# Last feed-forward part of a two-layer decoder: rows quantised by groups, rounding and conversion on ACT, tile stages spread over four steps

## The chip, the cores and the metric

The kernel runs on one core of a Trainium2 chip. The metric is the device time of one launch in microseconds (us), the median of several runs. One further execution was taken with the hardware profiler; all rows come from it.

## The reference

Two decoder layers work on x, 16 sequences of 64 rows of 256 columns in float32 (1024 rows). Layer 0 is a state-space block, a cross attention and a feed-forward part with two experts; layer 1 is an attention, a cross attention and the feed-forward part that the change touches. Each works on the layer norm of x and is added to x. The last one, with weights of 1024 x 256 (gate, up) and 256 x 1024 (down):

```
def _quant_weight(w):
    scale = mean(abs(w)) + EPS
    return clip(round(w / scale), -1, 1), scale
def _quant_act(x):
    s = max(abs(x), axis=-1) / 127 + EPS
    return clip(round(x / s), -128, 127), s
def _qlinear(x, w):
    wq, ws = _quant_weight(w);  xq, xs = _quant_act(x)
    return (xq @ wq.T) * xs * ws
h = silu(_qlinear(x, w_gate)) * _qlinear(x, w_up)
y = _qlinear(h, w_down)
```

## The kernel before, in words

Every engine has its own instruction list, written by hand; the engines meet only at semaphores. An instruction waits in its queue's order, and all that stands behind it on that engine waits too. `after(...)` on DVE and ACT makes the engine wait for its own instruction before the next. The 1024 rows lie in 8 tiles of 128 partitions (x[:, t, :]). PSUM has 8 banks of 2 KB a partition; `pair(a)` is banks a and a+1 as 1024 columns, `tiles2(a)` is bank a as two tiles of 256.

The last part begins where the second cross attention (`cross(1)`) ends. PE's project_out (L846) leaves two tiles each in banks 0 to 3 and signals x1_out once for each two.

Layer norm (`norm_rows(5, ...)`, DVE L1049 to L1063, ACT L380 and L381): for each group of two tiles DVE adds the bank to x, takes bn_stats and bn_aggr; ACT computes rstd with Ln and Exp; DVE scales group g-1 behind the statistics of group g.

Quantising the rows (DVE L1314 to L1323): once all 8 tiles are scaled, one maximum over all, two small instructions, a scale with minimum for each tile, one pass for maximum and adding MAGIC (1.5 x 2^23, which rounds), one pass for subtracting MAGIC and writing bf16, then the factors for gate and up (g_sc, u_sc). PE transposes (L1002) 8 tiles in two banks, ACT copies them out (L620) to t_xqT.

The tile loop runs over t from 0 to 8. In step t:
- PE (L1015): gate into pair(0), up into pair(2), 8 matmuls of 512 columns, once t_gate and t_prod say that tile t-1 has left these banks. Then for tile t-1: 8 transposes (L1022) of t_hq into bank 4, and after ACT's copy (t_hT) 8 down matmuls (L1029) into bank 5 or 6.
- ACT: Silu of the gate (L629), then the copy of bank 4 of tile t-1 to t_hqT (L633).
- DVE: product (L1330), maximum (L1334), its scale and reciprocal (L1335, L1336), scale with minimum (L1337), maximum and add MAGIC (L1338), subtract MAGIC to bf16 (L1341), down factor (L1342), and for tile t-1 the update of x from the down bank (L1345), which signals y_done.
- SP (L315) stores tile t of x on y_done.

In front of all this, weights t_gate, t_up and t_down have been loaded (DVE's 3 sums L1294) and quantised on POOL, long before. The kernel opens with four memsets on DVE. L426, L385 and L591 are ACT instructions of earlier parts.

## Time and profile before

| | us |
|---|---|
| median of 3 runs (lowest, highest) | 1158.2 (1157.13, 1160.88) |
| profiled execution, its own time | 1162.1 |
| its span | 1160.2 |
| PE, matmuls busy | 957.1 (82%) |
| DVE busy | 647.7 (56%) |
| ACT busy | 422.1 (36%) |
| POOL busy | 248.7 (21%) |

The span is what the trace shows from its first to its last event. Busy shares are averages over stages with different limits. In the rows, PE is the matmuls, PEld the weight loads, and the granted clock is a share of TensorE's full 2.4 GHz (0.50 is 1.2 GHz). `[2.69 <-DVE region_c L1330]` means that the engine had stood idle for 2.69 us and that this line's result ended it.

### The profile page before, as it was taken

What the parts mean: (1) busy time and instruction counts of PE and PEld (TensorE: products, weight loads), DVE (VectorE), ACT (ScalarE), POOL (GpSimd) and SP (SyncE); (2) the same over time, 40 slices, a digit from 0 to 9 for tenths busy, and PEclk for the clock granted to TensorE, in tenths of its full rate; (3) what the DMA queues carried; (4) which work ended last, traced back from release to release, by engine and by line L of the source; (5) the groups of instructions that cost most, each with busy time, mean ns of one, the idle gap of its engine ahead of it and who ended that gap; (6) DMA issues with size and microseconds to landing.
All of it is one profiled execution on the core that took longest, in us unless ns stands there. A gap on an engine that the chain in (4) does not pass through costs nothing.

```text
span 1160.2 us, 13033 instructions
## 1 busy us (share of the span) xinstructions
PE 957.1 (82%) x5454; PEld 597.4 (51%) x5458; DVE 647.7 (56%) x744; ACT 422.1 (36%) x632; POOL 248.7 (21%) x90
## 2 busy tenths in 40 slices
PE   4587787877879999999998999978863789999565
PEld 2133232322255566676666666647752467777332
DVE  2588789889942422333234344427768444444586
ACT  2653544542324655555452111142320313222232
POOL 0057586686600000000000000010009900000000
PEclk9788899988999999999998899987565989999777
DMA  8345454454614000000000500020000000000000
GB/s 304 86 128 141 108 146 130 109 145 125 183 62 174 1 1 1 1 1 1 1 1 1 208 0 1 1 108 3 3 5 0 1 1 1 1 1 2 0 14 23
DMA packets 17018, 64.43 MB, mean 56 GB/s; under 512 B 2848, under 2 KB 4512, under 8 KB 15456
## 3 DMA queue, kind: packets, MB, share of 16 engines
q1 hardware_dynamic: 16960, 63.60, 18.0%
q8 instruction: 43, 0.70, 0.3%
q14 instruction: 15, 0.12, 0.0%
HBM read 60.05 MB, written 3.15 MB: 54 GB/s over the span
## 4 chain that ended last, share of the span: by engine, by line
PE 63%; DVE 20%; ACT 7%; POOL 4%; issue 4%; DMA 1%; SPq 1%; DVEq 0%; POOLq 0%; ACTq 0%
PE ps L782 9%; PE ps L846 9%; DVE region_c L1138 6%; PE ps L888 5%; PE ps L702 5%; PE ps L898 5%; PE ps L657 4%; PE ps L814 3%; PE ps L836 3%; POOL region_c L347 3%; PE ps L800 3%; DVE ps L1133 2%; PE ps L796 2%; ACT region_c L565 2%; PE ps L789 1%
## 5 line engine op out<-in xcount | busy, mean ns | idle before, releaser
L702 PE MATMUL ps<-region_c,ident 128*128 128x512 f32 x256 | 141.4, 679 | 34.1 <-POOL region_c L347 25.0
L1138 DVE TENSOR_TENSOR_SCAN region_c<-region_c,ps 128x1024 f32<-128x1024 f32 x64 | 146.3, 2286 | 10.5 <-ACT region_c L470 8.5
L347 POOL TENSOR_TENSOR region_c<-region_c,region_b 128x1024 f32<-128x1024 f32 x43 | 105.0, 2442 | 110.4 <-DVE region_c L1138 103.2
L846 PE MATMUL ps<-region_c 128*128 128x256 f32 x512 | 117.5, 384 | 2.7 <-ACT region_c L565 2.7
L846 PEld LDWEIGHTS ps<-region_c 128*128 128x128 f32 x512 | 98.4, 193 | 27.4 <-issue 11.5
L470 ACT ACTIVATE region_c<-region_c,a_log 128x1008 f32<-128x1008 f32 x64 | 71.6, 1131 | 86.1 <-DVE region_c L1138 84.1
L356 POOL TENSOR_TENSOR x<-x,region_a 128x2048 f32<-128x2048 f32 x1 | 4.5, 4507 | 443.4 <-DVE xn L1049 443.4
L702 PEld LDWEIGHTS ps<-region_c,ident 128*128 128x128 f32 x256 | 50.4, 210 | 94.6 <-issue 47.3
L1133 DVE TENSOR_TENSOR ps<-ps,region_c 128x1024 f32<-128x1024 f32 x64 | 78.9, 1233 | 23.4 <-PE ps L690 18.4
L1200 DVE TENSOR_TENSOR region_c<-region_c 128x512 f32<-128x512 f32 x32 | 22.2, 692 | 119.8 <-ACT region_c L540 119.8
L565 ACT ACTIVATE region_c<-ps 128x512 f32<-128x512 f32 x64 | 36.9, 597 | 117.6 <-PE ps L836 117.6
L690 PE MATMUL ps<-region_b,sel_b 96*128 96x512 bf16 x128 | 41.1, 404 | 38.3 <-DVE ps L1133 32.5
L782 PE MATMUL ps<-xnT,region_a 128*128 128x512 f32 x128 | 60.7, 618 | 0.8
L888 PE MATMUL ps<-xnT,region_b 128*128 128x512 f32 x128 | 61.3, 605 | 0.0
L898 PE MATMUL ps<-region_b,region_c 128*128 128x256 f32 x256 | 60.1, 379 | 0.0
L836 PE MATMUL ps<-region_b,ctxn 64*128 64x128 f32 x512 | 56.7, 291 | 4.0 <-DVE region_b L1204 1.9
L782 PE MATMUL ps<-xnT,region_c 128*128 128x512 f32 x128 | 58.0, 598 | 0.8
L898 PEld LDWEIGHTS ps<-region_b,region_c 128*128 128x128 f32 x256 | 48.6, 190 | 19.4 <-issue 14.4
L523 ACT ACTIVATE region_c<-ps 128x512 f32<-128x512 f32 x64 | 37.9, 594 | 54.1 <-PE ps L782 54.1
L347 POOL TENSOR_TENSOR region_c<-region_c 128x1024 f32<-128x1024 f32 x21 | 51.4, 2446 | 27.9 <-DVE region_c L1138 23.3
L836 PEld LDWEIGHTS ps<-region_b,ctxn 64*128 64x128 f32 x512 | 50.5, 193 | 8.7 <-ACT region_c L565 5.2
L690 PEld LDWEIGHTS ps<-region_b,sel_b 96*128 96x128 bf16 x128 | 10.6, 102 | 85.7 <-DVE ps L1133 59.8
(188 smaller groups left out, 1535.7 us busy)
## 6 DMA issues: line engine op xcount, KB each, us to landing
region_b<-m_rows SPq DMA_DIRECT2D x43, 512.0 KB, 4.5
region_c<-m_rows SPq DMA_DIRECT2D x21, 512.0 KB, 4.6
region_a<-in_x_wo SPq DMA_DIRECT2D x2, 2048.0 KB, 12.0
m_rows<-region_b SPq DMA_DIRECT2D x4, 512.0 KB, 5.4
region_a<-in_x_wq SPq DMA_DIRECT2D x1, 2048.0 KB, 9.5
region_b<-in_f_fc SPq DMA_DIRECT2D x1, 2048.0 KB, 8.2
region_b<-in_f_proj SPq DMA_DIRECT2D x1, 2048.0 KB, 12.6
region_a<-in_x_wqT SPq DMA_DIRECT2D x1, 2048.0 KB, 14.6
```

The costliest lines, as they stand in the source:

```text
L347: pool.tensor_tensor(m_hc[u % 2], m_h[u % 3], m_cb[u % 3], ALU.mult).then_inc(sem("m_hc"), 1)
L470: act.activation(m_da[n % 2][:, :, 1:S], m_delta[k % 2][:, :, 1:S], ACT.Exp, scale=a_log[:, k, n:n + 1]).then_inc(sem("m_da"), 1)
L565: act.activation(dst, b.rearrange("p (a j n) -> p a j n", a=2, j=2), ACT.Copy)\
L690: last = pe.matmul(ps[:, c, :], sel_b[:, u % 32, :], m_sb[:, u // 32, c * HALF:c * HALF + HALF], start=True, stop=True)
L702: last = pe.matmul(ps[:, 4 + c, :], ident[:, :], m_hc[n % 2][:, c * HALF:c * HALF + HALF], start=(n == 0), stop=(n == DST - 1))
L782: last = pe.matmul(b, w, xnT[:, k, c * HALF:c * HALF + HALF], start=(k == 0), stop=(k == KH - 1))
L836: last = pe.matmul(b[:, :, m, :], ctxn[64 * r:64 * r + 64, js, :], mov, start=True, stop=True)
L846: last = pe.matmul(tiles2(t // 2)[:, t % 2, :], o_T[:, a, 128 * t:128 * t + 128], wvo[:, 2 * i + a, :], start=(i == 0 and a == 0 and t % 2 ...
L888: last = pe.matmul(ps[:, 4 + n % 4, :], f_fc[:, k, HID * e + 128 * hb:HID * e + 128 * hb + 128], xnT[:, k, c * HALF:c * HALF + HALF], star ...
L898: last = pe.matmul(tiles2(2 * e + t // 2)[:, t % 2, :], f_act[n % 4][:, 128 * t:128 * t + 128], f_proj[:, HB * e + hb, :], start=(hb == 0 ...
L1133: dve.tensor_tensor(pair(2), pair(0), m_du, ALU.mult).then_inc(sem("m_dbu"), 1)
L1138: dve.tensor_tensor_scan(m_h[u % 3], m_da[n % 2].rearrange("p b t -> p (b t)"), pair(2), 0.0, ALU.mult, ALU.add).then_inc(sem("m_scan"), 1)
```

## The change

Front: the last layer norm is written out. Behind the statistics of group g DVE runs scaled_rows(g-1) (scale, maximum, scales, factors, for these two tiles) and, later, clipped_rows. Rounding is now an ACT activation: Identity with the row's reciprocal scale as multiplier and MAGIC as addend, both read from `small`. DVE clips between MAGIC - 128 and MAGIC + 127 in one instruction, and a second ACT activation subtracts MAGIC and writes bf16. PE transposes by groups of two tiles, into banks 4 to 7, ACT copies by groups.

Loop: it runs over s from 0 to 11. In step s, gate and up, Silu, product and maximum are of tile s, rounding and clip of tile s-1, conversion to bf16 of tile s-2, transposes of tile s-3, copy, down matmuls and update of tile s-4. t_hqT and t_r have two buffers each; bank 4 stays the only one for transposes, and PE waits for the copy of the tile before (t_hT) ahead of them. The diff, in which longer runs of removed lines (they stand in the kernel above) are cut:

```diff
--- before.py
+++ after.py
@@ -200,8 +200,9 @@
         t_gate = [view("C", 16 + 4 * i, [HID]) for i in range(2)]
         t_h = [view("C", 24 + 4 * i, [HID]) for i in range(2)]
         t_hq = [view("C", 32 + 2 * i, [HID], BF16) for i in range(2)]
-        t_hqT = view("C", 36, [HB, 128], BF16)
-        t_r = view("C", 40, [HID])
+        t_hqT = [view("C", 36 + 2 * i, [HB, 128], BF16) for i in range(2)]
+        t_r = [view("C", 40 + 4 * i, [HID]) for i in range(2)]
+        magic_col, unmagic_col = small[:, 40:41], small[:, 41:42]
 
         def tiles2(a):
 
@@ -614,23 +615,66 @@
             norm_rows(4)
             cross(1)
 
-            norm_rows(5, transposed=False)
-            for g in range(2):
+            def rounded_rows(g):
+                act.wait_ge(sem("t_xs"), g + 1)
+                for t in (2 * g, 2 * g + 1):
+                    last = act.activation(t_xr[:, t, :], xn[:, t, :], ACT.Identity, scale=small[:, 32 + t:33 + t],
+                                          bias=magic_col)
+                last.then_inc(sem("t_xr"), 1)
+
+            def small_rows(g):
+                act.wait_ge(sem("t_xc"), g + 1)
+                act.activation(t_xq[:, 2 * g:2 * g + 2, :], t_xr[:, 2 * g:2 * g + 2, :], ACT.Identity,
+                               bias=unmagic_col).then_inc(sem("t_xq"), 1)
+
+            def turned_rows(g):
                 act.wait_ge(sem("t_xtr"), g + 1)
-                act.activation(t_xqT[:, :, HALF * g:HALF * g + HALF],
-                               ps[:, 2 * g, :].bitcast(BF16).rearrange("p (k n) -> p k n", k=KH), ACT.Copy)\
+                act.activation(t_xqT[:, :, 256 * g:256 * g + 256],
+                               ps[:, 4 + g, 0:256].bitcast(BF16).rearrange("p (k n) -> p k n", k=KH), ACT.Copy)\
                     .then_inc(sem("t_xT"), 1)
-            for t in range(NT + 1):
-                if t < NT:
-                    act.wait_ge(sem("t_gu"), t + 1)
-                    act.wait_ge(sem("t_sc"), 1)
+
+            for g in range(4):
+                act.wait_ge(sem("ln_var"), 4 * 5 + g + 1)
+                r = rstd[:, 2 * g:2 * g + 2]
+                after(act.activation(r, mv[:, 2 * g:2 * g + 2, 1], ACT.Ln, bias=eps_col))
+                act.activation(r, r, ACT.Exp, scale=-0.5).then_inc(sem("ln_rstd"), 1)
+                if g >= 2:
+                    rounded_rows(g - 2)
+            for g in range(4 + 1):
+                if g < 4:
+                    small_rows(g)
+                if g < 2:
+                    rounded_rows(g + 2)
+                if g >= 1:
+                    turned_rows(g - 1)
+
+            for s in range(NT + 4):
+                if s < NT:
+                    act.wait_ge(sem("t_gu"), s + 1)
+                    act.wait_ge(sem("t_sc"), s // 2 + 1)
+                    if s >= 2:
+                        act.wait_ge(sem("t_prod"), s - 1)
+                    act.activation(t_gate[s % 2], pair(0), ACT.Silu, scale=small[:, 56 + s:57 + s])\
+                        .then_inc(sem("t_gate"), 1)
+                if 1 <= s <= NT:
+                    t = s - 1
+                    act.wait_ge(sem("t_hr"), t + 1)
                     if t >= 2:
-                        act.wait_ge(sem("t_prod"), t - 1)
...
+                        act.wait_ge(sem("t_hq"), t - 1)
+                    act.activation(t_r[t % 2], t_h[t % 2], ACT.Identity, scale=small[:, 80 + t:81 + t],
+                                   bias=magic_col).then_inc(sem("t_round"), 1)
+                if 2 <= s <= NT + 1:
+                    t = s - 2
+                    act.wait_ge(sem("t_clip"), t + 1)
+                    if t >= 2:
+                        act.wait_ge(sem("t_htr"), t - 1)
+                    act.activation(t_hq[t % 2], t_r[t % 2], ACT.Identity, bias=unmagic_col).then_inc(sem("t_hq"), 1)
+                if s >= 4:
+                    t = s - 4
+                    act.wait_ge(sem("t_htr"), t + 1)
+                    if t >= 2:
+                        act.wait_ge(sem("t_dn"), t - 1)
+                    act.activation(t_hqT[t % 2], ps[:, 4, :].bitcast(BF16).rearrange("p (k n) -> p k n", k=HB),
                                    ACT.Copy).then_inc(sem("t_hT"), 1)
 
 
@@ -994,39 +1038,44 @@
             pe.wait_ge(sem("t_ws"), 1)
             cross(1)
 
-            for g in range(2):
-                pe.wait_ge(sem("t_xq"), 1)
-                xt = ps[:, 2 * g, :].bitcast(BF16).rearrange("p (k n) -> p k n", k=KH)
+            for g in range(4):
+                pe.wait_ge(sem("t_xq"), g + 1)
+                xt = ps[:, 4 + g, 0:256].bitcast(BF16).rearrange("p (k n) -> p k n", k=KH)
                 for k in range(KH):
-                    for t in range(4):
-                        last = pe.transpose(xt[:, k, 128 * t:128 * t + 128],
-                                            t_xq[:, 4 * g + t, 128 * k:128 * k + 128], identb[:, :])
+                    for a in range(2):
+                        last = pe.transpose(xt[:, k, 128 * a:128 * a + 128],
+                                            t_xq[:, 2 * g + a, 128 * k:128 * k + 128], identb[:, :])
                 last.then_inc(sem("t_xtr"), 1)
-            pe.wait_ge(sem("t_xT"), 2)
             pe.wait_ge(sem("t_wq"), 3)
-            for t in range(NT + 1):
...
+            pe.wait_ge(sem("t_xT"), 4)
+            for s in range(NT + 4):
+                if s < NT:
+                    if s >= 1:
+                        pe.wait_ge(sem("t_gate"), s)
+                        pe.wait_ge(sem("t_prod"), s)
                     for o, w in ((0, t_gate_q), (2, t_up_q)):
                         for c in range(2):
                             for k in range(KH):
-                                last = pe.matmul(ps[:, o + c, :], t_xqT[:, k, 128 * t:128 * t + 128],
+                                last = pe.matmul(ps[:, o + c, :], t_xqT[:, k, 128 * s:128 * s + 128],
                                                  w[:, k, 512 * c:512 * c + 512], start=(k == 0), stop=(k == KH - 1))
                     last.then_inc(sem("t_gu"), 1)
-                if t >= 1:
-                    pe.wait_ge(sem("t_hq"), t)
+                if 3 <= s <= NT + 2:
+                    t = s - 3
+                    pe.wait_ge(sem("t_hq"), t + 1)
+                    if t >= 1:
+                        pe.wait_ge(sem("t_hT"), t)
                     ht = ps[:, 4, :].bitcast(BF16)
                     for k in range(HB):
-                        last = pe.transpose(ht[:, 128 * k:128 * k + 128], t_hq[(t - 1) % 2][:, 128 * k:128 * k + 128],
+                        last = pe.transpose(ht[:, 128 * k:128 * k + 128], t_hq[t % 2][:, 128 * k:128 * k + 128],
                                             identb[:, :])
                     last.then_inc(sem("t_htr"), 1)
-                    pe.wait_ge(sem("t_hT"), t)
-                    if t >= 3:
-                        pe.wait_ge(sem("y_done"), t - 2)
+                if s >= 4:
+                    t = s - 4
+                    pe.wait_ge(sem("t_hT"), t + 1)
+                    if t >= 2:
+                        pe.wait_ge(sem("y_done"), t - 1)
                     for k in range(HB):
-                        last = pe.matmul(ps[:, 5 + (t - 1) % 2, 0:D], t_hqT[:, k, :], t_down_q[:, k, :],
+                        last = pe.matmul(ps[:, 5 + t % 2, 0:D], t_hqT[t % 2][:, k, :], t_down_q[:, k, :],
                                          start=(k == 0), stop=(k == HB - 1))
                     last.then_inc(sem("t_dn"), 1)
 
@@ -1067,6 +1116,8 @@
                 scale(3)
 
             dve.memset(eps_col, EPS)
+            dve.memset(magic_col, MAGIC)
+            dve.memset(unmagic_col, -MAGIC)
             dve.memset(half_col, -0.5)
             dve.memset(thr_col, LOG1P_SPLIT)
             dve.memset(one_col, 1.0).then_inc(sem("ready"), 1)
@@ -1307,43 +1358,69 @@
             after(dve.tensor_scalar(mask_add, mask_f, 1.0, -NEG, ALU.subtract, ALU.mult))
             cross(1)
 
-            norm_rows(5, (sem("x1_out"), [1, 2, 3, 4]))
-            dve.wait_ge(sem("ln_xn"), 48)
             xs, xrs = small[:, 24:32], small[:, 32:40]
             g_sc, u_sc = small[:, 56:64], small[:, 64:72]
-            after(dve.tensor_reduce(xs, xn[:, :, :], AX.X, ALU.max, apply_absolute_value=True))
...
+
+            def scaled_rows(g):
+                c = slice(2 * g, 2 * g + 2)
+                dve.wait_ge(sem("ln_rstd"), 4 * 5 + g + 1)
+                for t in (2 * g, 2 * g + 1):
+                    last = dve.tensor_scalar(xn[:, t, :], x[:, t, :], mv[:, t, 0:1], rstd[:, t:t + 1],
+                                             ALU.subtract, ALU.mult)
+                after(last)
+                after(dve.tensor_reduce(xs[:, c], xn[:, c, :], AX.X, ALU.max, apply_absolute_value=True))
+                after(dve.tensor_scalar(xs[:, c], xs[:, c], 1.0 / 127.0, EPS, ALU.mult, ALU.add))
+                dve.reciprocal(xrs[:, c], xs[:, c]).then_inc(sem("t_xs"), 1)
+                dve.tensor_scalar(g_sc[:, c], xs[:, c], ws[:, 0:1], None, ALU.mult)
+                dve.tensor_scalar(u_sc[:, c], xs[:, c], ws[:, 1:2], None, ALU.mult).then_inc(sem("t_sc"), 1)
+
+            def clipped_rows(g):
+                c = slice(2 * g, 2 * g + 2)
+                dve.wait_ge(sem("t_xr"), g + 1)
+                dve.tensor_scalar(t_xr[:, c, :], t_xr[:, c, :], MAGIC + 127.0, MAGIC - 128.0, ALU.min, ALU.max)\
+                    .then_inc(sem("t_xc"), 1)
+
+            for g in range(4):
+                dve.wait_ge(sem("x1_out"), g + 1)
+                after(dve.tensor_tensor(x[:, 2 * g:2 * g + 2, :], tiles2(g), x[:, 2 * g:2 * g + 2, :], ALU.add))
+                for t in (2 * g, 2 * g + 1):
+                    last = dve.bn_stats(stats[:, t, :], x[:, t, :])
+                after(last)
+                for t in (2 * g, 2 * g + 1):
+                    last = dve.bn_aggr(mv[:, t, :], stats[:, t, :])
+                last.then_inc(sem("ln_var"), 1)
+                if g >= 1:
+                    scaled_rows(g - 1)
+                if g >= 3:
+                    clipped_rows(g - 3)
+            scaled_rows(3)
+            for g in range(1, 4):
+                clipped_rows(g)
             hs, hr, dn = small[:, 72:80], small[:, 80:88], small[:, 88:96]
-            for t in range(NT + 1):
...
+            dve.wait_ge(sem("t_sc"), 4)
+            for s in range(NT + 4):
+                if s < NT:
+                    h, c = t_h[s % 2], slice(s, s + 1)
+                    dve.wait_ge(sem("t_gate"), s + 1)
+                    if s >= 2:
+                        dve.wait_ge(sem("t_round"), s - 1)
+                    dve.scalar_tensor_tensor(out=h, in0=pair(2), scalar=u_sc[:, c], in1=t_gate[s % 2],
                                              op0=ALU.mult, op1=ALU.mult).then_inc(sem("t_prod"), 1)
-                    dve.wait_ge(sem("t_prod"), t + 1)
-                    c = slice(t, t + 1)
+                    dve.wait_ge(sem("t_prod"), s + 1)
                     after(dve.tensor_reduce(hs[:, c], h, AX.X, ALU.max, apply_absolute_value=True))
                     after(dve.tensor_scalar(hs[:, c], hs[:, c], 1.0 / 127.0, EPS, ALU.mult, ALU.add))
-                    after(dve.reciprocal(hr[:, c], hs[:, c]))
...
+                    dve.reciprocal(hr[:, c], hs[:, c]).then_inc(sem("t_hr"), 1)
                     after(dve.tensor_tensor(dn[:, c], hs[:, c], ws[:, 2:3], ALU.mult))
-                if t >= 1:
-                    dve.wait_ge(sem("t_dn"), t)
-                    dve.scalar_tensor_tensor(out=x[:, t - 1, :], in0=ps[:, 5 + (t - 1) % 2, 0:D],
-                                             scalar=dn[:, t - 1:t], in1=x[:, t - 1, :],
+                if 1 <= s <= NT:
+                    t = s - 1
+                    dve.wait_ge(sem("t_round"), t + 1)
+                    dve.tensor_scalar(t_r[t % 2], t_r[t % 2], MAGIC + 127.0, MAGIC - 128.0, ALU.min, ALU.max)\
+                        .then_inc(sem("t_clip"), 1)
+                if s >= 4:
+                    t = s - 4
+                    dve.wait_ge(sem("t_dn"), t + 1)
+                    dve.scalar_tensor_tensor(out=x[:, t, :], in0=ps[:, 5 + t % 2, 0:D],
+                                             scalar=dn[:, t:t + 1], in1=x[:, t, :],
                                              op0=ALU.mult, op1=ALU.add).then_inc(sem("y_done"), 1)
```

## Rows read from the trace of the kernel before

**Rows 1.** The chain of waits, from 1078 on: start us, us, what
```profile
1078.92 0.70 DVE x L1057
...
1088.36 2.30 DVE small L1314
...
1099.36 3.21 PE ps L1015 x7
...
1157.45 0.48 DVE x L1345
```

**Rows 2.** Groups by line and shape, last 110 us: busy, mean ns | idle before
```profile
L1330 DVE SCALAR_TENSOR_TENSOR region_c<-ps,small,region_c 128x1024 f32<-128x1024 f32 x8 | 10.2, 1281 | 12.6 <-ACT region_c L629 12.6
L1334 DVE TENSOR_REDUCE small<-region_c 128x1 f32<-128x1024 f32 x8 | 9.8, 1220 | 0.3
L629 ACT ACTIVATE region_c<-ps,small 128x1024 f32<-128x1024 f32 x8 | 8.9, 1114 | 29.6 <-PE ps L1015 29.6
L633 ACT ACTIVATE region_c<-ps 128x1024 bf16<-128x1024 bf16 x8 | 8.2, 1021 | 8.8 <-PE ps L1022 8.8
...
L1337 DVE TENSOR_SCALAR region_c<-region_c,small 128x1024 f32<-128x1024 f32 x8 | 6.0, 753 | 0.3
...
L1338 DVE TENSOR_SCALAR region_c<-region_c 128x1024 f32<-128x1024 f32 x8 | 5.6, 694 | 0.3
...
L1345 DVE SCALAR_TENSOR_TENSOR x<-ps,small,x 128x256 f32<-128x256 f32 x8 | 3.9, 484 | 3.6 <-PE ps L1029 3.3
...
L1336 DVE RECIPROCAL small<-small 128x1 f32<-128x1 f32 x8 | 1.3, 164 | 0.3
```

**Rows 3.** Three stretches: us, busy of PE, PEld, DVE, ACT, POOL, clock, DMA share, GB/s
```profile
1104.00:1106.00 2.00, 0.75 (x4) 0.42 (x5) 1.97 (x2) 0.00 (x0) 0.00 (x0) 1.00 0.00 0
1106.00:1116.00 10.00, 7.85 (x30) 3.60 (x28) 8.40 (x16) 2.14 (x2) 0.00 (x0) 0.51 0.01 4
1118.00:1129.00 11.00, 6.54 (x47) 3.84 (x48) 10.52 (x18) 3.81 (x4) 0.00 (x0) 1.00 0.03 12
```

**Rows 4.** Timeline of the loop: start us, us, engine, line, [idle before]
```profile
1105.25 2.77 PE L1015 MATMUL ps<-region_b,region_c 128*128 128x512 bf16 x8 [2.69 <-DVE region_c L1330]
...
1109.05 1.03 PE L1022 MATMUL ps<-identb,region_c 128*128 128x128 bf16 x8 [1.03 <-DVE region_c L1341]
...
1111.20 1.89 PE L1029 MATMUL ps<-region_b,region_c 128*128 128x256 bf16 x8 [1.12 <-ACT region_c L633]
...
1112.88 3.61 PE L1015 MATMUL ps<-region_b,region_c 128*128 128x512 bf16 x8
...
1116.53 1.11 ACT L629 ACTIVATE region_c<-ps,small 128x1024 f32<-128x1024 f32 x1 [5.38 <-PE ps L1015]
1117.54 1.02 ACT L633 ACTIVATE region_c<-ps 128x1024 bf16<-128x1024 bf16 x1
...
1122.90 0.62 PE L1022 MATMUL ps<-identb,region_c 128*128 128x128 bf16 x8 [1.52 <-DVE region_c L1341]
...
1124.64 1.05 PE L1029 MATMUL ps<-region_b,region_c 128*128 128x256 bf16 x8 [1.12 <-ACT region_c L633]
...
1125.52 1.89 PE L1015 MATMUL ps<-region_b,region_c 128*128 128x512 bf16 x8
```

**Rows 5.** Timeline of DVE in the last layer norm, additions of groups 2 and 3
```profile
1082.94 0.69 DVE L1057 TENSOR_TENSOR x<-ps,x 128x512 f32<-128x512 f32 x1
...
1085.23 0.68 DVE L1057 TENSOR_TENSOR x<-ps,x 128x512 f32<-128x512 f32 x1
```

**Rows 6.** Groups of ACT over the whole span, by shape: busy, mean ns | idle before
```profile
L426 ACT ACTIVATE region_a<-region_a,small 128x1024 f32<-128x1024 f32 x4 | 4.6, 1148 | 0.1
...
L385 ACT ACTIVATE xnT<-ps 128x512 f32<-128x512 f32 x20 | 11.2, 592 | 8.4 <-PE ps L644 8.3
...
L591 ACT ACTIVATE region_c<-ps,qb_half,parity 128x512 f32<-128x512 f32 x4 | 3.1, 778 | 5.5 <-PE ps L917 5.5
...
L629 ACT ACT_TABLE_LOAD x1 | 1.3, 1283 | 0.0
```

More of the change, by code:

```diff
@@ L619, in _ @@
+            def turned_rows(g):
                 act.wait_ge(sem("t_xtr"), g + 1)
-                act.activation(t_xqT[:, :, HALF * g:HALF * g + HALF],
-                               ps[:, 2 * g, :].bitcast(BF16).rearrange("p (k n) -> p k n", k=KH), ACT.Copy)\
+                act.activation(t_xqT[:, :, 256 * g:256 * g + 256],
+                               ps[:, 4 + g, 0:256].bitcast(BF16).rearrange("p (k n) -> p k n", k=KH), ACT.Copy)\
                     .then_inc(sem("t_xT"), 1)
-            for t in range(NT + 1):
-                if t < NT:
-                    act.wait_ge(sem("t_gu"), t + 1)
-                    act.wait_ge(sem("t_sc"), 1)
-                    if t >= 2:
-                        act.wait_ge(sem("t_prod"), t - 1)
-                    act.activation(t_gate[t % 2], pair(0), ACT.Silu, scale=small[:, 56 + t:57 + t])\
-                        .then_inc(sem("t_gate"), 1)
-                if t >= 1:
-                    act.wait_ge(sem("t_htr"), t)
-                    act.activation(t_hqT, ps[:, 4, :].bitcast(BF16).rearrange("p (k n) -> p k n", k=HB),
+            for g in range(4):
[5 more added lines that the diff above has]
+                    rounded_rows(g - 2)
@@ L1308, in _ @@
             cross(1)
-            norm_rows(5, (sem("x1_out"), [1, 2, 3, 4]))
-            dve.wait_ge(sem("ln_xn"), 48)
             xs, xrs = small[:, 24:32], small[:, 32:40]
             g_sc, u_sc = small[:, 56:64], small[:, 64:72]
-            after(dve.tensor_reduce(xs, xn[:, :, :], AX.X, ALU.max, apply_absolute_value=True))
-            after(dve.tensor_scalar(xs, xs, 1.0 / 127.0, EPS, ALU.mult, ALU.add))
-            after(dve.reciprocal(xrs, xs))
-            for t in range(NT):
-                ins = dve.tensor_scalar(t_xr[:, t, :], xn[:, t, :], xrs[:, t:t + 1], 127.0, ALU.mult, ALU.min)
@@ L1319, in _ @@
-            after(ins)
-            after(dve.tensor_scalar(t_xr, t_xr, -128.0, MAGIC, ALU.max, ALU.add))
-            dve.tensor_scalar(t_xq, t_xr, MAGIC, None, ALU.subtract).then_inc(sem("t_xq"), 1)
-            after(dve.tensor_scalar(g_sc, xs, ws[:, 0:1], None, ALU.mult))
-            dve.tensor_scalar(u_sc, xs, ws[:, 1:2], None, ALU.mult).then_inc(sem("t_sc"), 1)
-            dve.wait_ge(sem("t_sc"), 1)
-            hs, hr, dn = small[:, 72:80], small[:, 80:88], small[:, 88:96]
-            for t in range(NT + 1):
-                if t < NT:
-                    h = t_h[t % 2]
-                    dve.wait_ge(sem("t_gate"), t + 1)
-                    dve.scalar_tensor_tensor(out=h, in0=pair(2), scalar=u_sc[:, t:t + 1], in1=t_gate[t % 2],
+            def scaled_rows(g):
[10 more added lines that the diff above has]
+                dve.tensor_scalar(u_sc[:, c], xs[:, c], ws[:, 1:2], None, ALU.mult).then_inc(sem("t_sc"), 1)
@@ L1337, in _ @@
-                    after(dve.tensor_scalar(t_r, h, hr[:, c], 127.0, ALU.mult, ALU.min))
-                    after(dve.tensor_scalar(t_r, t_r, -128.0, MAGIC, ALU.max, ALU.add))
-                    if t >= 2:
-                        dve.wait_ge(sem("t_htr"), t - 1)
-                    dve.tensor_scalar(t_hq[t % 2], t_r, MAGIC, None, ALU.subtract).then_inc(sem("t_hq"), 1)
-                    after(dve.tensor_tensor(dn[:, c], hs[:, c], ws[:, 2:3], ALU.mult))
-                if t >= 1:
-                    dve.wait_ge(sem("t_dn"), t)
-                    dve.scalar_tensor_tensor(out=x[:, t - 1, :], in0=ps[:, 5 + (t - 1) % 2, 0:D],
-                                             scalar=dn[:, t - 1:t], in1=x[:, t - 1, :],
+                    dve.reciprocal(hr[:, c], hs[:, c]).then_inc(sem("t_hr"), 1)
```

4 lines of the change are left out of this document (removed).

## The prediction

> **What bounds the kernel now.** The profiled execution took 1162.1 us, a span of 1160.2 us and 1.9 us around it; the three timed runs have a median of 1158.2 us, 3.9 us less. The sum below is made against the profiled execution, and its difference is then laid on the median. The runs shown differ by 3.75 us, so I call 0.3% (3.5 us) what a measurement of this kernel can tell from no change.
>
> First I read the chain of waits at its end [rows 1]. The last cross attention hands over its first pair of tiles at 1078.92. From there until the last update of x at 1157.93 (1157.45 plus 0.48) the chain runs through the last feed-forward part, and the last 2.3 us are the output transfer, which the change leaves alone. So only 79 us of 1160 can move. They fall in two stages.
>
> The **front** (1078.92 to 1099.36): layer norm, then the quantisation of all eight tiles on DVE, one instruction behind another, then transposes and copies, then the first gate matmul. The **loop** (1099.36 to 1157.93, 58.6 us for eight tiles): matmuls, Silu, product, maximum, three quantising passes, transposes, copy, down matmuls.
>
> Then I read the groups of instructions [rows 2]. Per tile DVE has a product of 1.28 us, a maximum of 1.22, three small ones of 0.16, three passes (0.75, then 0.69, the third, to bf16, like the second), and the update of 0.48: 5.6 us with its small gaps. ACT has only Silu (1.11) and a copy (1.02). DVE sets the pace where PE runs at full clock; where it doesn't, PE does. The clock view and the timeline show both [rows 3, 4]: gate and up matmuls of one tile take 3.4 us at half clock (1.2 GHz) and 1.8 at full clock (2.4 GHz), since their records of 3.61 and 1.89 start 0.2 us before the work ahead of them ends; transposes take 1.03 or 0.62, down matmuls 1.89 or 1.05.
>
> **Part 1, the front.** Before, layer norm groups came every 2.29 us on DVE [rows 5]. The new scaled_rows puts behind each a maximum over 512 columns (half of 1.22 plus a start-up, 0.69, with its gap 0.72), three or four small instructions (0.19, 0.10, 0.10, 0.10) and a wait more (0.1): some 1.3 us. So groups come every 3.6 us. Group 0 has no scaled_rows (1.72), groups 1 and 2 take 3.6 each, group 3 takes 1.7 and 2.0, then comes a clip (0.45) and the last scaled_rows (2.0): DVE reaches its second clip at 1094.0. On ACT a rounding over 256 columns has no row. Its nearest are the copy of 512 columns at 0.59 [rows 6], less half of the 0.43 by which 1024 columns cost more (1.02, rows 2), plus 0.09 for each of two pointer operands (0.775 against 0.592 in rows 6 is 0.18 for two): 0.56. Below it is 0.38 (pointers free), above 0.77, the whole row with pointers. Two of these are 1.1 us a group, the conversion of 512 columns with one pointer 0.7, the turned copy 0.6. ACT's queue order then is rounded(2), convert(1), rounded(3), turned(0), convert(2), turned(1), convert(3), turned(2), turned(3). A clip of 512 columns takes about 0.4, so convert(1) starts near 1094.4. The six jobs up to convert(3) add 0.7 + 1.1 + 0.6 + 0.7 + 0.6 + 0.7, less five overlaps of 0.10 (part 2), and end at 1098.3; then transposes 0.6 and copy 0.6 give 1099.5, and the first matmul starts 0.45 later, as now. That is 1099.95 against 1099.36: **plus 0.6 us**. What DVE no longer does in one piece (2.30 for the maximum alone, rows 1) comes back as more, smaller instructions in front and as an ACT queue behind. The bounds are minus 1.0 (pointers free and no extra gaps) and plus 2.5 (0.77 per rounding on both late groups, and each wait a little longer). Two memsets at the kernel's start cost about 0.1 us while DVE waits for x's first rows to arrive; the gain and the loss there are nothing, and without that cover they cost that 0.1.
>
> **Part 2, what each engine has per tile in the loop.** DVE loses the passes of 0.75 and 0.69 and keeps one clip of 0.69: 1.28 + 1.22 + 0.48 + 0.69 and three small ones, 4.3 us with gaps. ACT gains rounding and conversion over 1024 columns from SBUF. L426 is such an instruction with one pointer, 1.15 us [rows 6]; the conversion takes that as it is, the rounding with 0.09 more, 1.24. Bounds for each are 1.02 and 1.33. With Silu and copy, and 0.10 of overlap between neighbours (a copy starts at 1117.54 while Silu ends at 1117.64, rows 4), ACT has 4.2 us. The DVE queue and ACT's would each allow a tile every 4.3 us.
>
> **Part 3, the order of the waits.** Here the loop fails to reach that. Transposes of tile s-3 write the one bank 4, so PE now waits for the copy of tile s-4 (t_hT) ahead of them. ACT issues that copy as its last job of step s, behind Silu(s), rounding(s-1) and conversion(s-2). And Silu(s) waits for gate and up of tile s, which PE issues ahead of those same transposes. Queued on PE behind the wait are the transposes, the down matmuls, and gate and up of tile s+1, for which Silu(s+1) waits. So from step 4 on one step is a closed ring with nothing beside it: gate/up + 4.2 of ACT + transposes + down + four hand-overs of 0.04. DVE's work lies inside ACT's 4.2 and PE's burst.
> At full clock that is 1.8 + 4.2 + 0.62 + 1.05 + 0.15 = 7.8 us; at half clock 3.42 + 4.2 + 1.04 + 1.89 + 0.15 = 10.7 us. Per tile, 58.6 us over eight is 7.3 before, drain and fill included.
>
> Steps 0 to 3 have no such wait: gate/up + Silu + product + hops, 4.3 us at full, 5.9 at half clock, four of them. Then three rings bring tile 7's gate matmuls; these and ACT's 4.2 follow (6.0 or 7.6). The drain behind copy(3): rounding(7), conversion(6), copy(4) 3.2; conversion(7) and copy(5) 2.1; then transposes and copy in turn for tiles 6 and 7, with down(6) off the path, then down(7) and the update: 5.0 at full clock, 6.7 at half. Together 10.3 or 12.0.
> Full clock throughout: 17.2 + 23.4 + 6.0 + 10.3 = **56.9 us**. Half clock throughout: 23.6 + 32.1 + 7.6 + 12.0 = **75.3 us**. Before: 58.6.
>
> **Part 4, which clock.** In the trace the granted clock fell to half within 1 us after PE's idle time of 2.69 us (1.00 in 1104 to 1106, 0.51 from 1106 to 1116), and it rose only behind 3.2 us of unbroken work (from 1099.36) or some 5 us of it (1111.20 to 1116.49) [rows 1, 3, 4]. The ring leaves PE idle for 4.2 us in every step, longer than that 2.69. So I take it that each burst starts at half clock and that about its last 1.8 us of half-clock work run at full: 6.35 becomes 5.4, the ring 9.8. With early steps mostly at half clock (22.7), three rings (29.4), 7.0 and a drain of 11.0 the loop is 70.1 us. Plus 0.6 in front: 70.7 against 58.6, **12.1 us more**. On the profiled execution's own time 1174.2; on the median **1170.3**.
> The Trainium skill ("TensorE: Matmul & The Clock Gate", section "HAM oscillation — how this bites in real kernels") describes a loop whose waits let the clock fall in every turn, so that each burst starts slow. By that rule the sum is 1170; if a burst of this size kept the clock up it would be 57.5 for front and loop, 1157. The row from 1106 is on the rule's side; that from 1118 to 1129 is not, but there PE's idle time comes in two pieces a tile.
>
> **Rivals.**
> Full clock throughout: 56.9 + 0.6 - 58.6 is minus 1.1, 1157.1, no change. For it: full clock for 11 us (1118 to 1129, rows 3) with PE busy 59% of the time. Against: in the ring it is 3.5 of 7.8 us, 45%, and the idle time is in one piece. 0.10.
> Half clock throughout: 75.3 + 0.6 - 58.6 is plus 17.3, 1175.5. For it: 0.51 from 1106 to 1116 with PE busy 7.85 of 10 us [rows 3]. 0.17.
> Faster: the pace of the busiest engine. If the ring isn't closed (the copy of tile s-4 done by the time PE comes to transposes s-3, which needs ACT's jobs behind Silu to end within gate/up and DVE's time), tiles come every 4.4 us: 3.4 + 7 x 4.4 + 1.1 and one tile's way through all stages, 10.0, is 45.3; with 0.6 in front minus 12.7, 1145.5. It decides once the copy ends within 4.4 us of the last one. For it: every engine has under 4.4 us a tile. Against: the order of the two queues leaves no such slack. 0.06.
> A table reload: if the rounding's function were not in Silu's table set, two loads of 1.28 [rows 6] would stand in each ACT step, 2.6 us in each of three rings and one more step, 10 us or more: 1181 and up. The copies between Silus need none, and only one load stands in that loop now. 0.04. The Trainium skill ("ScalarE: Activation LUTs", section on table sets) lists identity among the functions that every set has, and puts a switch at 2.66 us with its drain; by that figure such a rival would cost double.
>
> **How the numbers follow.** The forecast case (each burst part slow) has 0.63: with clock, front and ACT bounds it spans 1165 to 1175. The range reaches from 1161, half way towards the full-clock case, to 1178, the half-clock case with the front's upper bound. Left out are full clock (0.10), the faster rival (0.06) and the reload (0.04). Slower by over 0.3%: 0.63 + 0.17 + 0.04, less a little for a milder mixture, 0.83; within 0.3% 0.10; faster 0.07.
>
> **What would show it.** In the changed profile: first gate matmul near 1100; rounding 1.24 and conversion 1.15 us; DVE 4.3 us a tile and idle between; gate matmuls of tiles 5 to 7 starting about 10 us apart, each burst preceded by an idle PE that waited for the copy on ACT; the clock near 0.5 at its start. I am wrong if those starts are under 7 us apart, if a table load stands between Silu and rounding, or if the front has moved by over 3 us.

## The result, and the profile after

The changed kernel takes 1169.26 us, the median of four runs (1166.0 to 1172.18); four runs of the kernel before gave 1158.52. The ratio is 1.009, with a 95% interval of 1.0055 to 1.0125: slower, by under one per cent. The profiled execution took 1171.09 us, a span of 1169.3. Two executions of later runs fell far outside the others (1646 us at a mean clock of 0.58 in the version with two banks, 3179 us at 1.00 in the kernel before) and enter no ratio.

The stages of the end, by the chain of waits (start us, us, what), changed kernel:

```profile
1075.28 0.70 DVE x L1385
...
1095.40 0.61 ACT region_c L632
...
1155.15 0.14 issue
...
1166.53 0.48 DVE x L1422
```

The first addition of the last layer norm starts at 1075.28, the last copy of quantised rows ends at 1096.01, the last update of x at 1167.01. I use these three marks from here on, for they need no matmul record. Front: 20.7 us, against 20.0 before (1078.92 to 1098.92). Loop: 71.0 us against 59.0. The tail stays at 2.3 us. So the last feed-forward part lost 12.7 us, while all stages ahead of it came out 3.6 us shorter (75.28 against 78.92), though the change touches nothing there but two memsets.

The groups by line and shape (busy us, mean ns | idle before), to be held against [rows 2, 6]:

```profile
L1407 DVE SCALAR_TENSOR_TENSOR region_c<-ps,small,region_c 128x1024 f32<-128x1024 f32 x8 | 10.3, 1284 | 25.7 <-ACT region_c L657 25.7
L664 ACT ACTIVATE region_c<-region_c,small 128x1024 f32<-128x1024 f32 x8 | 9.8, 1230 | 0.0
L1410 DVE TENSOR_REDUCE small<-region_c 128x1 f32<-128x1024 f32 x8 | 9.8, 1220 | 0.3
L671 ACT ACTIVATE region_c<-region_c,small 128x1024 bf16<-128x1024 f32 x8 | 9.1, 1139 | 1.3 <-PE ps L1069 1.3
L657 ACT ACTIVATE region_c<-ps,small 128x1024 f32<-128x1024 f32 x8 | 8.9, 1113 | 31.2 <-PE ps L1059 31.2
L677 ACT ACTIVATE region_c<-ps 128x1024 bf16<-128x1024 bf16 x8 | 8.1, 1010 | 1.6 <-PE ps L1069 1.6
...
L1417 DVE TENSOR_SCALAR region_c<-region_c 128x1024 f32<-128x1024 f32 x8 | 5.5, 692 | 0.2
...
L1422 DVE SCALAR_TENSOR_TENSOR x<-ps,small,x 128x256 f32<-128x256 f32 x8 | 3.9, 484 | 14.9 <-PE ps L1078 14.9
...
L621 ACT ACTIVATE region_c<-xn,small 128x256 f32<-128x256 f32 x8 | 4.3, 584 | 0.0
...
L627 ACT ACTIVATE region_c<-region_c,small 128x512 bf16<-128x512 f32 x4 | 2.9, 715 | 1.5 <-DVE region_c L1380 1.5
...
L657 ACT ACT_TABLE_LOAD x1 | 1.3, 1283 | 0.0
```

Rounding (L664) takes 1.23 us, conversion (L671) 1.14, rounding of 256 columns (L621) 0.58. DVE lost two passes a tile and now waits 25.7 us for Silu in front of its product, where it had waited 12.6. One table load remains, ahead of the loop.

The timeline of step 4, and Silu of the three steps behind it:

```profile
1118.54 1.89 PE L1059 MATMUL ps<-region_b,region_c 128*128 128x512 bf16 x8 [1.91 <-DVE region_c L1407]
...
1120.47 1.11 ACT L657 ACTIVATE region_c<-ps,small 128x1024 f32<-128x1024 f32 x1 [1.22 <-PE ps L1059]
1121.48 1.23 ACT L664 ACTIVATE region_c<-region_c,small 128x1024 f32<-128x1024 f32 x1
...
1122.61 1.14 ACT L671 ACTIVATE region_c<-region_c,small 128x1024 bf16<-128x1024 f32 x1
...
1123.65 1.01 ACT L677 ACTIVATE region_c<-ps 128x1024 bf16<-128x1024 bf16 x1
...
1124.80 1.01 PE L1069 MATMUL ps<-identb,region_c 128*128 128x128 bf16 x8 [4.37 <-ACT region_c L677]
...
1125.61 1.91 PE L1078 MATMUL ps<-region_b,region_c 128*128 128x256 bf16 x8
...
1130.57 1.11 ACT L657 ACTIVATE region_c<-ps,small 128x1024 f32<-128x1024 f32 x1 [5.92 <-PE ps L1059]
...
1140.75 1.11 ACT L657 ACTIVATE region_c<-ps,small 128x1024 f32<-128x1024 f32 x1 [5.98 <-PE ps L1059]
...
1150.95 1.11 ACT L657 ACTIVATE region_c<-ps,small 128x1024 f32<-128x1024 f32 x1 [6.02 <-PE ps L1059]
```

Read it as one ring. Gate and up of tile 4 end at 1120.4 and Silu starts. ACT then works without a gap through Silu, rounding and conversion to the copy, which ends at 1124.66. PE has stood idle for 4.37 us and its record names the copy; then come transposes, down matmuls, gate and up of the next tile. Silu to Silu is 10.1, 10.2 and 10.2 us. Windows of the same stretch (us, busy of PE, PEld, DVE, ACT, POOL, clock, DMA share, GB/s):

```profile
1120.50:1150.90 30.40, 16.91 (x70) 9.35 (x72) 12.49 (x22) 12.54 (x12) 0.00 (x0) 0.66 0.04 13
1122.00:1124.00 2.00, 0.00 (x0) 0.00 (x0) 1.97 (x2) 2.00 (x3) 0.00 (x0) 0.80 0.00 0
1124.00:1126.00 2.00, 1.20 (x10) 1.14 (x11) 1.22 (x5) 0.66 (x1) 0.00 (x0) 0.50 0.00 0
1128.00:1130.00 2.00, 2.00 (x6) 0.73 (x5) 0.04 (x1) 0.00 (x0) 0.00 (x0) 0.50 0.19 66
```

The clock falls while PE waits (0.80 on average in 1122 to 1124), is at 0.50 when the burst begins and still is in 1128 to 1130. Over the three rings it is 0.66, and neither DVE nor ACT is busy for half of the time.

### The profile page after: what moved, and what is told of

It reads as the page before. It is cut to its first block, busy times and chain, and to the rows that moved or that the text cites. A ratio compares the mean times of both kernels' runs of the same rounds, so it can differ in the third digit from the quotient of the medians.

```text
span 1169.3 us, 13084 instructions
## 1 busy us (share of the span) xinstructions
PE 953.4 (82%) x5455; PEld 591.5 (51%) x5458; DVE 634.8 (54%) x739; ACT 445.6 (38%) x662; POOL 248.8 (21%) x90
## 4 chain that ended last, share of the span: by engine, by line
PE 62%; DVE 18%; ACT 9%; issue 4%; POOL 4%; DMA 2%; SPq 1%; DVEq 0%; POOLq 0%; ACTq 0%
PE ps L826 9%; PE ps L890 9%; DVE region_c L1189 5%; PE ps L932 5%; PE ps L746 5%; PE ps L942 5%; PE ps L701 3%; PE ps L880 3%; POOL region_c L348 3%; PE ps L858 3%; PE ps L844 2%; DVE ps L1184 2%; PE ps L840 2%; PE ps L1059 2%; ACT region_c L566 2%
## 5 line engine op out<-in xcount | busy, mean ns | idle before, releaser
L580 ACT ACTIVATE region_c<-region_c 128x512 f32<-128x512 f32 x32 | 20.1, 629 | 89.1 <-DVE region_c L1285 89.1
L734 PEld LDWEIGHTS ps<-region_b,sel_b 96*128 96x128 bf16 x128 | 10.6, 101 | 85.7 <-DVE ps L1184 60.0
## 6 DMA issues: line engine op xcount, KB each, us to landing
region_a<-in_x_wqT SPq DMA_DIRECT2D x1, 2048.0 KB, 14.4
```

What stands on the lines that cost most here:

```text
L734: last = pe.matmul(ps[:, c, :], sel_b[:, u % 32, :], m_sb[:, u // 32, c * HALF:c * HALF + HALF], start=True, stop=True)
```

## The experiments

Eleven kernels were run, one of them twice. The kernel before, measured in the same rounds, had medians of 1159.8 to 1160.0 us. The changed kernel was not measured again in them; beside its 1169.3 the kernel before had 1158.5. So "us under the changed kernel" compares medians of different rounds; held against the kernel before of the same rounds, each such difference is 1.3 to 1.5 us larger. Loop and front are between the marks above, each from one profile, and do not depend on that.

| kernel | median us | ratio to before (95%) | front | loop |
|---|---|---|---|---|
| before | 1158.5 to 1160.0 | | 20.0 | 59.0 |
| changed | 1169.3 | 1.009 (1.0055 to 1.0125) | 20.7 | 71.0 |
| copy first | 1147.8 | 0.9869 (0.9838 to 0.99) | 20.7 | 50.7 |
| copy second | 1154.9 | 0.996 (0.9937 to 0.9982) | 20.7 | 59.3 |
| two banks | 1163.9 | 1.0014 (0.9987 to 1.004) | 20.7 | 65.7 |
| PE filled | 1161.5 | 1.0003 (0.9981 to 1.0026) | 20.7 | 65.2 |
| new front, old loop | 1154.0 | 0.9923 (0.9894 to 0.9953) | 20.7 | 55.8 |
| old front, new loop | 1168.0 | 1.0062 (1.0039 to 1.0085) | 20.0 | 71.8 |
| memsets only | 1155.4 | 0.996 (0.9939 to 0.9982) | 20.0 | 59.0 |
| before again | 1159.6 | 0.9998 (0.9974 to 1.0021) | 20.0 | 58.0 |
| copy first, split waits | 1141.1 | 0.9843 (0.9811 to 0.9875) | 20.7 | 42.5 |
| and two banks | 1135.1 | 0.9793 (0.9766 to 0.9821) | 20.7 | 40.4 |
| and warm front | 1135.2 | 0.9813 (0.9766 to 0.986) | 20.5 | 39.2 |

### Which loop, which front

The old front with the new loop (ACT, PE and DVE loops of the changed kernel, `t_sc` counted once):

> The front of the kernel before with the new tile loop (and the two memsets). Theory (the whole loss lies in the loop's ring): 9 to 14 us over the kernel before, loop of 69 to 72 us in the profile. Rival (loop and front cost only together): under 6 us over it.

1168.0 us, 8.2 over the kernel before, a little under the 9 to 14 expected; the loop is 71.8, as expected. Against the kernel with the memsets only it is 12.6 us in medians and 12.8 in the loop. The loss lies in the loop.

The new front with the old loop:

> The new front (rows quantised by groups behind the layer norm, rounding and conversion on ACT) with the loop of the kernel before. Theory: the front gives nothing, 0.6 to 0.8 us more from the first addition of the last layer norm to the first gate matmul, so within 3 us of the kernel before and some 10 us under the changed kernel. Rival (the front costs a good part of the 11 us): 4 us or more over the kernel before.

The profile gives the front the 0.7 us more that were expected, and the changed kernel is 15.3 us over it, in medians as in the loop (some 10 were expected). But its median is 5.9 us **under** the kernel before, outside the 3 us that I had allowed. Its loop, the same instructions as before, took 55.8 us at a clock of 0.84 (first line), where the same loop in the kernel before took 59.0 at 0.79 (second line):

```profile
1092.80:1148.50 55.70, 33.77 (x192) 17.55 (x192) 43.65 (x72) 18.25 (x17) 0.00 (x0) 0.84 0.05 17
```

```profile
1098.90:1157.90 59.00, 35.79 (x188) 18.56 (x192) 43.82 (x72) 18.07 (x18) 0.00 (x0) 0.79 0.05 16
```

and the stages ahead of it were 6.9 us shorter. The two runs that follow are for that.

### The order of ACT's jobs

Copy first (the block of the copy, five lines, moves as it is):

```diff
             for s in range(NT + 4):
+                if s >= 4:
...
                 if s < NT:
                     act.wait_ge(sem("t_gu"), s + 1)
...
-                if s >= 4:
...
```

> The changed kernel, with one move on ACT: the copy of tile s-4 stands ahead of Silu(s) in step s instead of last. No instruction more or less. Theory (closed ring): the copy then no longer hangs on gate and up of tile s, PE's transposes and down matmuls find their data waiting, and a step falls from 10.1 us (gate matmuls, then 4.2 us of ACT, then transposes and down matmuls) to what ACT's 4.3 us or the chain gate/up + Silu + product allow, 4.4 to 5.9 us. Three rings less 4 to 5 us each and a shorter drain: 15 to 21 us under the changed kernel, 1149 to 1155, under the kernel before as well. Rival (the added ACT work and its amount cost the time, not its order): same time as the changed kernel within 3 us.

1147.8 us, with the same instructions on every engine: 21.4 us under the changed kernel, just beyond the 15 to 21 expected; the loop alone is 20.3 us shorter. Its PE timeline (L1069 are the transposes):

```profile
1124.11 1.89 PE L1059 MATMUL ps<-region_b,region_c 128*128 128x512 bf16 x8 [1.27 <-DVE region_c L1407]
1125.86 0.61 PE L1069 MATMUL ps<-identb,region_c 128*128 128x128 bf16 x8
1126.31 1.04 PE L1078 MATMUL ps<-region_b,region_c 128*128 128x256 bf16 x8
1128.61 1.89 PE L1059 MATMUL ps<-region_b,region_c 128*128 128x512 bf16 x8 [1.26 <-DVE region_c L1407]
...
1133.11 1.89 PE L1059 MATMUL ps<-region_b,region_c 128*128 128x512 bf16 x8 [1.27 <-DVE region_c L1407]
```

Gate matmuls come 4.50 us apart, at full clock, transposes and down matmuls follow them without a wait, and only DVE's product ends PE's idle time. The ring is open; the rival, in which the amount of work on ACT costs the time, falls.

Copy second, the same move to the place right behind Silu:

> The changed kernel with the copy of tile s-4 behind Silu(s), but ahead of rounding and conversion. Theory (ring of gate/up, ACT's jobs up to the copy, transposes, down matmuls): the ring loses the 2.2 us of rounding and conversion, PE's idle time in a step falls from 4.4 to 2.2 us and some bursts keep full clock; three rings and the first steps of the drain give 7 to 12 us less than the changed kernel, between that and the version with the copy first (1148). Rival (the ring is opened as soon as the copy isn't last): same as the version with the copy first within 2 us.

```profile
1127.91 0.78 PE L1069 MATMUL ps<-identb,region_c 128*128 128x128 bf16 x8 [2.21 <-ACT region_c L664]
...
1130.19 2.59 PE L1059 MATMUL ps<-region_b,region_c 128*128 128x512 bf16 x8
...
1137.51 2.35 PE L1059 MATMUL ps<-region_b,region_c 128*128 128x512 bf16 x8
```

Gate matmuls start 6.1, 7.3 and 7.3 us apart (those of tile 4 ran at full clock, the later ones only in part), and PE waits 2.21 us for the copy (L664 in this kernel), where it had waited 4.37. So the ring still exists and is shorter by the jobs taken out of it (2.2 us) and by a faster burst (4.9 us against 5.8). The loop is 11.7 us shorter than in the changed kernel, at the top of the 7 to 12 expected, the median 14.4, which is outside them. It is 7 us over the copy first, so the rival falls.

### The bank

```diff
                     if t >= 2:
-                    if t >= 1:
-                        pe.wait_ge(sem("t_hT"), t)
-                    ht = ps[:, 4, :].bitcast(BF16)
+                        pe.wait_ge(sem("t_hT"), t - 1)
+                    ht = ps[:, 4 + 3 * (t % 2), :].bitcast(BF16)
```

(and the same bank in ACT's copy).

> The changed kernel, with transposes alternating between banks 4 and 7, so that PE waits at them for the copy two tiles back, not one. Theory (closed ring): only the transposes (1.0 us at half clock) and a hand-over leave the ring, since the down matmuls of tile s-4 stand next on PE and wait for the same copy; 3 to 5 us under the changed kernel. Rival (the single bank alone closes the ring, as one would read from the wait at the transposes): the ring opens and it is 12 us or more under it.

5.4 us under the changed kernel, just above the forecast of 3 to 5, and far from the rival's 12. The profile that is read here, with a loop 5.3 us shorter, comes from one more execution:

> The two-bank version once more, for a profile: the first one was taken in an execution at half clock almost throughout. Theory (the down matmuls keep the ring closed): in each ring PE goes from gate and up straight to the transposes, then stands idle about 3.4 us for ACT's copy ahead of the down matmuls, and gate matmuls of tiles 5 to 7 start 8.5 to 9.5 us apart, against 10.1. Rival (the single bank closed the ring): no such idle time and under 7 us.

```profile
1132.70 1.89 PE L1078 MATMUL ps<-region_b,region_c 128*128 128x256 bf16 x8 [3.79 <-ACT region_c L677]
1134.38 3.62 PE L1059 MATMUL ps<-region_b,region_c 128*128 128x512 bf16 x8
1137.79 1.01 PE L1069 MATMUL ps<-identb,region_c 128*128 128x128 bf16 x8
1142.29 1.89 PE L1078 MATMUL ps<-region_b,region_c 128*128 128x256 bf16 x8 [3.48 <-ACT region_c L677]
```

Transposes now follow gate and up at once. PE waits for the copy ahead of the down matmuls, 3.8 and 3.5 us here (3.4 expected), and the last gate matmuls start 9.6 us apart (1134.38, 1143.97), a little over the 8.5 to 9.5 expected. The wait that one sees named in the changed kernel (the transposes', for the one bank) is only the first of two on the same copy; taking it away moved the wait by eight instructions.

### The clock

```diff
                     last.then_inc(sem("t_gu"), 1)
+                if 3 <= s < NT:
+                    for c in range(8):
+                        pe.matmul(ps[:, 7, :], t_xqT[:, 0, 0:128], t_gate_q[:, 0, 0:512], start=True, stop=True)
                 if 3 <= s <= NT + 2:
```

> The changed kernel, with 8 added matmuls of 512 columns into the unused bank 7 behind gate and up in steps 3 to 7 (their results are not used); at half clock they take 3.4 us, less than the 4.2 us for which PE waits there. Theory (the wait costs a second time, through the clock): with PE kept busy the transposes, down and gate/up matmuls run at full clock, a ring falls from 10.1 towards 7.9 us, in all 4 to 9 us under the changed kernel in spite of more work. Rival (the clock does not depend on this wait): no change, or 0 to 3 us slower.

7.8 us under the changed kernel, 5.9 of them in the loop, with 40 matmuls more. One ring of it (L1064 are the added matmuls, L1072 the transposes), and the window over the stretch of the rings:

```profile
1123.42 1.89 PE L1059 MATMUL ps<-region_b,region_c 128*128 128x512 bf16 x8
1125.14 1.89 PE L1064 MATMUL ps<-region_b,region_c 128*128 128x512 bf16 x8
1129.68 0.61 PE L1072 MATMUL ps<-identb,region_c 128*128 128x128 bf16 x8 [2.65 <-ACT region_c L677]
...
1131.27 3.30 PE L1059 MATMUL ps<-region_b,region_c 128*128 128x512 bf16 x8
```

```profile
1118.00:1146.50 28.50, 17.94 (x103) 9.17 (x102) 15.32 (x28) 16.65 (x17) 0.00 (x0) 0.94 0.04 14
```

Gate matmuls are 7.6 us apart where the burst ran at full clock, and 7.9 and 9.0 where it fell within it; the clock averaged 0.94 against 0.66. So of a ring of 10.2 us some 7.6 are the dependence itself and up to 2.6 are what its idle time costs through the clock.

### Versions under both kernels

Split waits, on top of the copy first:

```diff
-                        pe.wait_ge(sem("t_gate"), s)
-                        pe.wait_ge(sem("t_prod"), s)
                     for o, w in ((0, t_gate_q), (2, t_up_q)):
+                        if s >= 1:
+                            pe.wait_ge(sem("t_prod" if o else "t_gate"), s)
...
-                    last.then_inc(sem("t_gu"), 1)
+                        last.then_inc(sem("t_u" if o else "t_g"), 1)
```

(ACT's Silu waits for t_g, DVE's product for t_u as well.)

> The changed kernel with the copy ahead of Silu, and PE's two waits split: gate matmuls wait only for Silu of the tile before, up matmuls only for its product; Silu starts on gate alone, the product also waits for up. Theory (with the ring gone a step is the chain gate/up + Silu + product, 4.50 us at full clock and 5.9 at half): the chain falls under ACT's and DVE's own work per tile, about 4.3 us at either clock; four early steps gain up to 1.5 us each and later ones 0.1 to 0.2, in all 4 to 7 us under the version with the copy moved alone. Rival (the pace is already that of ACT and DVE): 0 to 2 us under it.

6.7 us less than with the copy alone, at the top of what was expected; the loop is 8.1 us shorter.

> The version before this one with transposes alternating between banks 4 and 7. Theory (with the copy first in each ACT step the wait for the one bank is met before PE comes to it, save in the drain): 0 to 2 us under that version. Rival (the single bank still holds PE back in each step): 4 us or more under it.

6.0 us less in medians, but only 2.1 in the loop; the rest lies in the stages ahead, whose length varies from run to run. The profile bears out the theory, the median by itself would have spoken for the rival. At 1135.1 us this version is 25 us under the kernel before and 34 under the changed one, with all of the changed kernel's arithmetic. What bounds it in its steady steps:

```profile
1106.00:1122.00 16.00, 12.57 (x90) 6.83 (x90) 15.45 (x28) 16.00 (x17) 0.00 (x0) 1.00 0.07 25
```

ACT is busy for 16.00 of 16 us, DVE for 15.45, at full clock. That is the pace of the busiest engine, 4.08 us a tile.

> The version with copy first, split waits and two banks, with nine matmuls of 512 columns added between the transposes of the front (4, 3, 1 and 1, into bank 0, their results are not used), where PE waits for ACT. Theory (the first gate and up matmuls run at half clock because PE stands idle through the front): they then run at full clock, the loop starts 1.5 to 3 us shorter, 1132 to 1134. Rival (the added matmuls delay the transposes or the clock still isn't granted): no gain, or up to 1 us slower.

The window over the end of its front, and its first gate and up matmuls:

```profile
1092.00:1099.00 7.00, 4.99 (x26) 2.17 (x27) 2.51 (x9) 6.33 (x13) 0.00 (x0) 0.76 0.00 0
```

```profile
1098.87 1.28 ACT L664 ACT_TABLE_LOAD   x1
...
1098.91 1.90 PE L1060 MATMUL ps<-region_b,region_c 128*128 128x512 bf16 x8 [0.47 <-ACT region_c L632]
1100.17 1.11 ACT L664 ACTIVATE region_c<-ps,small 128x1024 f32<-128x1024 f32 x1
...
1101.38 1.28 DVE L1409 SCALAR_TENSOR_TENSOR region_c<-ps,small,region_c 128x1024 f32<-128x1024 f32 x1 [5.33 <-ACT region_c L664]
```

The first burst ran at full clock, 1.9 us, as meant. The loop became 1.2 us shorter, less than the 1.5 to 3 expected. The profile shows where it stops: the first product starts 2.5 us behind the front's last copy, against 3.7 in the version without the added matmuls, and it now waits for Silu, which starts as soon as the table load ends. From the second product on the distance stays 1.2 us. The median did not move (1135.2), so this one is inconclusive as to its worth. (From the end of the copy, 1098.86, to the start of Silu this table load takes 1.31 us in all; the 2.66 us that the prediction quotes for a switch do not appear here.)

### What the stages ahead do

> The kernel before with only the two added memsets at its start. The new front with the old loop came out 0.8% under the kernel before, though its profile shows no gain in the front (20.9 us against 20.4) and only 3 us in the loop; the rest lay ahead of both, in stages that the change leaves alone. Theory (the stages ahead vary from run to run with the clock, and no part of the change acts on them): within 3 us of the kernel before. Rival (the two memsets shift all that follows against the clock, and those stages gain from it): 3 us or more under it.

> The kernel before, unchanged, measured as if it were a changed one. It tells what this measurement makes of no change. With the two added memsets alone the time came out at 0.996 of it (0.9939 to 0.9982). If the interval of this run leaves out 1 by as much, that 0.4% is the measurement's own; if it holds 1 and the cross attention of layer 0 takes 295 us in the profile as in the two others without the new front or loop, the cause of the difference stays open.

The kernel before against itself: 0.9998 (0.9974 to 1.0021), with runs from 1154.2 to 1161.9. The memsets alone: 0.996, its interval ends at 0.9982, and its one profile shows the cross attention of layer 0 as long as in the kernel before (295.0 us against 295.2); but that profile fell on the slowest of its twelve runs (1164.9 us) and says little about the others. The two intervals overlap. So it is over 3 us under it in the medians, as the rival had it. The mean granted clock of each execution speaks for the rival too: with the two memsets it was 0.900 or more in 11 of 12 executions, in the kernel before of the same rounds in 1 of 17. The one profile is of the exception (0.892). So chance alone is an unlikely account; in which stages the memsets act, and how, stays open.

## Why the prediction was right, point by point

The forecast was 1170.3 us with a range of 1161 to 1178; measured were 1169.3. By its steps:

- **Front, plus 0.6 us.** Plus 0.7 between the marks. Layer norm groups came 3.66 us apart (3.6 forecast), rounding of 256 columns took 0.58 (0.56), conversion 0.72 (0.7), copies 0.58 (0.6). One reading was wrong and cost nothing: the 0.45 us ahead of the first gate matmul are a missing record (x7 in [rows 1], where eight are issued). In the second profile of the kernel before, where all eight are there, the first starts 0.05 us behind the copy.
- **ACT, 4.2 us a tile in the ring.** 1120.47 to 1124.66 is 4.19.
- **The ring, 9.8 us.** 10.1 to 10.2. The hand-over from ACT's copy to PE was 0.14 and not 0.04, and the burst took 5.7 to 5.8 us where I had 5.4: the clock rose later in it.
- **Early steps 22.7, three rings 29.4, last ring's part 7.0, drain 11.0, sum 70.1.** By starts of gate matmuls and the copy's end: 22.5, 29.3, 7.3 and 11.9, sum 71.0.
- **The clock.** At half at each start of a burst. The filled version shows cause and price, which the forecast had only argued: without the fall a ring is 7.6 us, where the full-clock rival had 7.8.
- **The rivals.** Full clock throughout: the clock was 0.66 in the rings. Half clock throughout: the drain and some early bursts were faster. A table reload: one load, ahead of the loop. The pace of the busiest engine: it did not come, but it is what the loop does once the ring is open. The forecast gave 4.4 us a tile and a loop of 45.3 us for it, from the first gate matmul to the last update; the version with two banks has 4.08 and 40.4.
- **What the forecast did not hold.** The last part lost 12.7 us, the medians differ by 10.7 and the profiles' spans by 9.1, since the stages ahead were 3.6 us shorter in the profile. The forecast took those stages as fixed and put the two memsets at nothing; the kernel with the memsets alone came out 4.4 us under the kernel before. Two errors, the last part 0.6 us too cheap and the stages ahead too long, cancel in part, and that the forecast lies within 1.1 us of the median is partly luck.

## What to carry to other kernels

When stages are spread over more steps, write down for each engine the order of its jobs within one step and follow the waits around: if the last job of engine A gates a job of B that stands ahead of the one which releases A's first job, the depth of the pipeline buys nothing, and a step costs the sum of all of them. The profile named only the first of two waits on this ring; move the job (here the oldest tile's, ahead of the youngest's) and not the wait. And look at the clock behind an idle time of TensorE that recurs in each step: here 4.37 us of it were paid twice, since the burst behind it started at half clock, while the 1.27 us in the later steps of the copy-first version left the gate and up matmuls at full clock (1.89 us).

## What the runs showed of the hardware that was not expected

The stages which no variant touches vary by several us between profiles, and the clock goes with it. The cross attention of layer 0 (us, busy of the engines, clock) in the kernel before and in the changed one:

```profile
333.60:628.80 295.20, 281.86 (x1673) 191.19 (x1672) 97.99 (x135) 148.07 (x276) 0.00 (x0) 0.95 0.05 19
```

```profile
337.70:622.30 284.60, 271.27 (x1674) 182.43 (x1673) 97.97 (x135) 147.90 (x276) 0.00 (x0) 0.99 0.05 19
```

The same 1670 or so matmuls take 295.2 us at a mean clock of 0.95, or 284.6 at 0.99. The kernel before in a second profile took 291.0, seven of the variants 284.6 to 284.7, one 287.1, two 293.8 and 295.0. Only the pair of the kernel before compares one kernel with itself; the 284.6 came in eight of eleven profiles with the two memsets at the kernel's start and in neither without them, so part of this can belong to the kernels and not to chance. Ten microseconds, as much as the change itself, hang on how the clock stands in one stage, so a profile of one execution says what a change did only between marks of the stage it touches. The Trainium skill ("TensorE: Matmul & The Clock Gate", section "The HAM clock gate") says that what one kernel pays at the gate varies from run to run; the two profiles of the kernel before agree, 295.2 and 291.0 us at 0.95 and 0.97. It also puts the penalty of the ramp at under 1% of a typical kernel's span. No run here isolates the ramp; the 10.6 us between the two profiles shown are 0.9% of the span, in one stage alone.
